# Scan stage: segment decays turned round into two fp32r parts made on GpSimd, input products in three fp32r passes

## What is computed

```python
u = layernorm(u, x_norm_w, x_norm_b)                       # after the adaptive norm
zxbcdt = einsum('bld,od->blo', u, l2norm(in_proj_w)) * DIM ** -0.5
z, xBC, dt_raw = zxbcdt[..., :512], zxbcdt[..., 512:1152], zxbcdt[..., 1152:]
xBC = silu(causal_conv(xBC, conv_w, taps=4) + conv_b)      # x: 4 heads of 128, B and C: 64 each
dt = softplus(dt_raw + dt_bias);  A = -exp(A_log)
# per chunk
dA = dt * A;  cum = cumsum(dA)
decay[i, j] = exp(cum[i] - cum[j])  for j <= i, per head
y = (C B^T * decay * dt) x  +  C state exp(cum)  +  D x
state = state * exp(cum[-1]) + B^T (dt * exp(cum[-1] - cum) * x)
g = y * silu(z);  out = rmsnorm(g) @ l2norm(out_proj_w).T
```

## Time and profile before

| | |
|---|---|
| median of 3 runs | 5127.16 us (5111.26 to 5134.68) |
| span of the profiled execution | 5138.9 us |
| attention | 262.7 to 2922.3 us |
| first mixture | 2928.5 to 3606.2 us |
| scan, with its set-up | 3618.3 to 4510.0 us |
| route and second mixture | 4516.0 to 5130.7 us |
| busy over the span | PE 92%, DVE 83%, ACT 68%, POOL 27% |

### The profile page before, as it was taken

How to read it: one execution, slowest core, us unless ns; L and a number is a source line. 1 busy time by engine, 2 the same in 40 slices (tenths; PEclk the granted TensorE clock), 3 DMA queues, 4 the chain that set the end, 5 groups by cost and what they waited for, 6 DMA issues and landing times. The chain is left out here.

```text
span 5138.9 us, 109366 instructions
## 1 busy us (share of the span) xinstructions
PE 4706.1 (92%) x35413; PEld 2589.8 (50%) x35413; DVE 4275.5 (83%) x6882; ACT 3471.8 (68%) x6677; POOL 1377.0 (27%) x1279
## 2 busy tenths in 40 slices
PE   5869999999999999999999689999599999955998
PEld 4723333333333333333333267777366666645887
DVE  5779999999999999999999768878677877775554
ACT  2428888888888888888888523223377877734554
POOL 1111111111111111111111133333234443435776
PEclk8969999999999999999999889999699999956999
DMA  4931222212222122221222211111100000044442
GB/s 153 349 67 35 52 52 46 43 35 53 52 46 43 35 53 51 46 43 38 50 54 43 71 40 37 41 45 37 53 21 27 25 23 28 21 156 164 166 160 92
DMA packets 236717, 340.13 MB, mean 66 GB/s; under 512 B 60215, under 2 KB 170034, under 8 KB 227612
## 3 DMA queue, kind: packets, MB, share of 16 engines
q1 hardware_dynamic: 220032, 275.39, 22.3%
q0 software_dynamic: 16192, 58.43, 3.1%
HBM read 205.62 MB, written 136.18 MB: 67 GB/s over the span
## 5 line engine op out<-in xcount | busy, mean ns | idle before, releaser
L719 DVE TENSOR_REDUCE at_mxp<-at_ps_m 128x2 f32<-128x1024 f32 x2092 | 2524.4, 1221 | 70.2 <-PE at_ps_m L772 47.3
L692 ACT ACTIVATE at_prob<-at_ps_s 128x512 f32<-128x512 f32 x4100 | 2227.3, 596 | 323.5 <-PE at_ps_s L762 299.7
L782 PE MATMUL at_ps_o<-at_prob,at_vs 128*32 128x256 f32 x16384 | 1313.1, 392 | 13.9 <-ACT at_osum L698 13.9
L762 PE MATMUL at_ps_s<-at_qs,at_ks 51*128 51x512 f32 x4100 | 1036.7, 500 | 2.7 <-ACT at_prob L692 2.7
L772 PE MATMUL at_ps_m<-at_ks,at_qs 49*128 49x512 f32 x4184 | 859.0, 406 | 49.8 <-DMA at_ks<-t_alibi 34.4
L762 PEld LDWEIGHTS at_ps_s<-at_qs,at_ks 51*128 51x128 f32 x4100 | 384.6, 183 | 853.3 <-ACT at_prob L692 852.8
L782 PEld LDWEIGHTS at_ps_o<-at_prob,at_vs 128*32 128x32 f32 x16384 | 322.9, 108 | 778.2 <-issue 389.7
L564 POOL TENSOR_TENSOR at_total<-at_total,at_minus 128x16 f32<-128x16 f32 x65 | 189.6, 2917 | 1128.4 <-DMA at_total<-at_osum 1128.4
L772 PEld LDWEIGHTS at_ps_m<-at_ks,at_qs 49*128 49x128 f32 x4184 | 403.7, 190 | 73.7 <-DVE at_mxp L719 38.0
L67 DVE TENSOR_TENSOR ex_hidc<-ex_hid,ex_hidc 128x512 fp32r<-128x512 f32 x128 | 158.5, 1250 | 169.6 <-ACT ex_hid L2550 169.6
L1222 PE MATMUL mi_ps_f<-mi_w,mi_act 128*128 128x256 f32 x1024 | 260.1, 399 | 17.4 <-DVE mi_acc L1072 17.1
(11 more groups left out here) (317 smaller groups left out, 6161.6 us busy)
## 6 DMA issues: line engine op xcount, KB each, us to landing
t_parts<-pr_parts SPq DMA_DIRECT2D x64, 512.0 KB, 6.4
ex_w<-in_fw SPq DMA_DIRECT2D x32, 1024.0 KB, 7.4
at_ks<-t_parts SPq DMA_DIRECT2D x102, 256.0 KB
t_buf<-at_blank POOLq DMA_DIRECT2D x64, 384.5 KB, 3.2
at_qs<-t_parts SPq DMA_DIRECT2D x96, 256.0 KB
at_vs<-t_v SPq DMA_DIRECT2D x17, 1024.0 KB, 4.8
ex_rest<-t_buf SPq DMA_DIRECT2D x16, 1026.0 KB, 5.2
t_v<-pr_vaug SPq DMA_DIRECT2D x64, 256.0 KB, 5.6
```

The costliest lines, as they stand in the source:

```text
L692: nc.scalar.activation(prob[0 if up is None else (t + 1) % 2][:, j, :], ps_s[bank][:, :], ACT.Exp).then_inc(s_read, 1)
L719: nc.vector.tensor_reduce(out[:, s4, k + i, 2 * pair:2 * pair + 2], ps_m[i][:, :, :], AX.X, ALU.max).then_inc(mx_read, 1)
L762: nc.tensor.matmul(ps_s[bank][:, :], ks[s][a:a + QROWS, j // 2, t1 * P:(t1 + 1) * P], qs[s][a:a + QROWS, j // 2, c * T:(c + 1) * T], start ...
L782: last = nc.tensor.matmul(ps_o[32 * j:32 * j + 32, q0:q1], vs[s][:, t, 32 * j:32 * j + 32], prob[t % 2][:, j, q0:q1], start=(t == 0 and ha ...
```

## The change

1. **Decays** (`segment_mask`, `decays`). The roles of the factors are turned round: `lowerc`, an fp32r copy of `lower`, is stationary, and the moving factor is `upper * dA` for all four heads side by side, 512 columns. It is made in two fp32r parts from an upper and a lower part of `dA` (`step_parts`, five drains and four small operations). The masks move from ACT (four 128x128 operations) to GpSimd (two 128x512 operations). TensorE then does two fp32r matmuls of 512 columns in place of four fp32 ones of 128.
2. **Gates and convolution inputs.** `uTc[h]` and `winc` hold fp32r upper and lower parts. Each of the 18 products per turn of 512 columns is three fp32r passes. ACT now writes both `uTc[h][0]` and the fp32 `uT` (one buffer, read by `steps`); GpSimd makes the lower part (`lower_rows`). The weights are cut once, in the set-up: ACT the upper parts, GpSimd the lower.
3. **In place.** The convolution works in `xs[h]`; the tile `cv` is gone.

The diff, cut to its core:

```diff
-        win = sb("win", [P, KD, ZX])
+        wdt = sb("wdt", [P, KD, NH])
+        winc = [sb(f"winc{c}", [P, KD, RT * P], F32R) for c in range(2)]
...
-        uT = [sb(f"uT{h}", [P, KD, T]) for h in range(2)]
+        uT = sb("uT", [P, KD, T])
+        uTc = [[sb(f"uTc{h}{c}", [P, KD, T], F32R) for c in range(2)] for h in range(2)]
...
-        cv = sb("cv", [P, CTL, T])
...
+                def step_parts(h):
+                    pool.drain()
+                    nc.gpsimd.tensor_scalar(dA_big[:, :, :], dA[h][:, :, :], 4097.0, None, ALU.mult)
+                    pool.drain()
+                    nc.gpsimd.tensor_tensor(dA_off[:, :, :], dA_big[:, :, :], dA[h][:, :, :], ALU.subtract)
+                    pool.drain()
+                    nc.gpsimd.tensor_tensor(dAc[h][0][:, :, :], dA_big[:, :, :], dA_off[:, :, :], ALU.subtract)
+                    pool.drain()
+                    lower_part(nc.gpsimd, dAc[h][1][:, :, :], dA[h][:, :, :], dAc[h][0][:, :, :])
+                    pool.drain()
+
+                def segment_mask(h, s, used):
+                    if used is not None:
+                        pool.wait_ge(a_done, used + 1)
+                    for c in range(2):
+                        last = nc.gpsimd.tensor_tensor(segc[s % 2][c][:, :, :], upper[:, :].unsqueeze(1).to_broadcast([P, NH, P]),
+                                                       over_h(dAc[h][c][:, s, :].bitcast(F32)), ALU.mult)
+                    last.then_inc(seg_set, 1)
+
+                def lower_rows(turn, h, k, name):
+                    pool.wait_ge(a_out, place(turn, name)[0] + 1)
+                    lower_part(nc.gpsimd, uTc[h][1][:, k, :], uT[:, k, :], uTc[h][0][:, k, :]).then_inc(u_cut, 1)
...
                         second_root(i + 2)
+                        segment_mask(h, 3, place(turn, "seg1")[0])
                         if c == 0:
                             weigh_rows(b, i)
                         softplus_argument(i + 1)
                         softplus_series(i + 1, 1 - h)
                         gate(i, h, 1, old)
+                        step_parts(1 - h)
+                        segment_mask(1 - h, 0, place(turn, "seg2")[0])
                         gate(i, h, 2, True)
+                        segment_mask(1 - h, 1, place(turn, "seg3")[0])
                         gate(i, h, 3, True)
+                        lower_rows(turn, h, 0, "uT0")
+                        segment_mask(1 - h, 2, place(turn, "seg0")[0])
+                        lower_rows(turn, h, 1, "uT1")
...
-                    for k in range(NH):
-                        last = nc.scalar.activation(segm[s % 2][:, k, :], lower[:, :], ACT.Copy, scale=dA[h][:, s, k:k + 1])
-                    last.then_inc(seg_set, 1)
...
-                    nc.scalar.activation(uT[h][:, k, :], bank[:, :], ACT.Identity, scale=nw[:, k:k + 1], bias=nb[:, k:k + 1]).then_inc(a_out, 1)
+                    nc.scalar.activation(uTc[h][0][:, k, :], bank[:, :], ACT.Identity, scale=nw[:, k:k + 1], bias=nb[:, k:k + 1])
+                    nc.scalar.activation(uT[:, k, :], bank[:, :], ACT.Identity, scale=nw[:, k:k + 1], bias=nb[:, k:k + 1]).then_inc(a_out, 1)
...
+                act.wait_ge(w_read, 5)
+                for j in range(5):
+                    nc.scalar.copy(win_part(0, j), win_f[j]).then_inc(win_upper, 1)
...
+                    if ct == 4:
+                        pe.wait_ge(u_cut, KD if i is None else KD * (i[0] + 2))
...
-                        last = nc.tensor.matmul(bank[:, :], win[:, k, DI + ct * P:DI + (ct + 1) * P], uT[h][:, k, :], start=(k == 0), stop=(k == KD - 1))
+                        for n, (a, r) in enumerate(CUTS):
+                            last = nc.tensor.matmul(bank[:, :], winc[a][:, k, DI + ct * P:DI + (ct + 1) * P], uTc[h][r][:, k, :],
+                                                    start=(k == 0 and n == 0), stop=(k == KD - 1 and n == 2))
...
-                    for k in range(NH):
-                        last = nc.tensor.matmul(bank[:, k * P:(k + 1) * P], segm[s % 2][:, k, :], upper[:, :], start=True, stop=True)
+                    for c in range(2):
+                        last = nc.tensor.matmul(bank[:, :], lowerc[:, :], segc[s % 2][c][:, :, :].rearrange("p h c -> p (h c)"), start=(c == 0), stop=(c == 1))
```

More of the change, by code:

```diff
@@ L1319, in scan_phase @@
         two = lambda name, shape: [sb(f"{name}{h}", shape) for h in range(2)]
-        segm, decay, att = two("segm", [P, NH, P]), two("decay", [P, NH, P]), two("att", [P, NH, P])
+        decay, att = two("decay", [P, NH, P]), two("att", [P, NH, P])
+        segc = [[sb(f"segc{h}{c}", [P, NH, P], F32R) for c in range(2)] for h in range(2)]
+        dAc = [[sb(f"dAc{h}{c}", [P, SUB, NH], F32R) for c in range(2)] for h in range(2)]
+        dA_big, dA_off = sb("dA_big", [P, SUB, NH]), sb("dA_off", [P, SUB, NH])
+        lowerc = sb("lowerc", [P, P], F32R)
         sm, btw, ex = two("sm", [P, P]), two("btw", [P, NH, NS]), two("ex", [P, 3, SUB, NH])
@@ L1356, in scan_phase @@
         RND = 7
+        WIN_PIECES = [(8, 9), (4, 6), (6, 8), (0, 2), (2, 4)]
+        win_part = lambda c, j: winc[c][:, :, WIN_PIECES[j][0] * P:WIN_PIECES[j][1] * P]
+        win_f = [(osb[0] if j == 0 else sz[1])[:, :, :].rearrange("p s c -> p (s c)")[:, a % 8 * D:a % 8 * D + KD * (b - a) * P].rearrange("p (k c) -> p k c", k=KD)
+                 for j, (a, b) in enumerate(WIN_PIECES)]
         over_h = lambda v: v.unsqueeze(2).to_broadcast([P, NH, P])
@@ L1471, in batch @@
                         h = c % 2
+                        turn = (i, c)
                         old = c > 0 or not first
@@ L1493, in _ @@
                 second_root(0)
+                for j in range(3):
+                    lower_weights(j)
                 first_root(1)
+                for k in range(KD):
+                    lower_rows(None, 0, k, f"uT{k}")
+                for j in range(3, 5):
+                    lower_weights(j)
                 pool.wait_ge(setup_v, 3)
@@ L1498, in _ @@
                 second_root(1)
+                pool.wait_ge(const_in, NCONST)
+                step_parts(0)
+                segment_mask(0, 0, None)
+                segment_mask(0, 1, None)
+                for k in range(KD):
+                    lower_rows(None, 1, k, f"vT{k}")
+                segment_mask(0, 2, place(None, "seg0")[0])
                 pool.wait_ge(w_read, RND)
-                pool.wait_ge(const_in, NCONST)
                 batch(0, True)
@@ L1693, in _ @@
                 dve.wait_ge(const_in, NCONST)
+                nc.vector.tensor_copy(lowerc[:, :], lower[:, :]).then_inc(lower_cut, 1)
                 for r in range(RND):
@@ L1842, in batch @@
                         steps(turn)
-                        segment_mask(i, h, 3, place(turn, "seg1")[0])
                         decays(turn, i, 1, old)
@@ L1858, in batch @@
                         decays(turn, i, 3, True)
-                        segment_mask(i + 1, 1 - h, 0, place(turn, "seg2")[0])
                         projected(turn, h, 0)
@@ L1864, in batch @@
                         decays(turn, i + 1, 0, True)
-                        segment_mask(i + 1, 1 - h, 1, place(turn, "seg3")[0])
                         gates(turn, 1 - h, 2)
@@ L1881, in batch @@
                         projected(turn, h, 3)
-                        segment_mask(i + 1, 1 - h, 2, place(turn, "seg0")[0])
                         skip_inputs(turn, i + 1, 1 - h, 0, True)
@@ L1909, in conv_inputs @@
                 def conv_inputs(i, h, ct):
+                    if i is None:
+                        pe.wait_ge(win_cut, {4: 1, 0: 2, 1: 2, 2: 3, 3: 3}[ct])
+                    if ct == 4:
+                        pe.wait_ge(u_cut, KD if i is None else KD * (i[0] + 2))
                     bank = into(i, f"ct{ct}")
                     for k in range(KD):
[L1912 removed]
+                        for n, (a, r) in enumerate(CUTS):
+                            last = nc.tensor.matmul(bank[:, :], winc[a][:, k, DI + ct * P:DI + (ct + 1) * P], uTc[h][r][:, k, :],
+                                                    start=(k == 0 and n == 0), stop=(k == KD - 1 and n == 2))
                     last.then_inc(a_done, 1)
                 def gates(i, h, s):
+                    if i is None:
+                        pe.wait_ge(win_cut, 5)
                     bank = into(i, f"z{s}")
                     for k in range(KD):
[L1918 removed]
+                        for n, (a, r) in enumerate(CUTS):
+                            last = nc.tensor.matmul(bank[:, :], uTc[h][a][:, k, s * P:(s + 1) * P], winc[r][:, k, 0:DI],
+                                                    start=(k == 0 and n == 0), stop=(k == KD - 1 and n == 2))
                     last.then_inc(a_done, 1)
@@ L1924, in steps @@
                         for k in range(KD):
-                            last = nc.tensor.matmul(bank[:, s * NH:(s + 1) * NH], uT[h][:, k, s * P:(s + 1) * P], win[:, k, RT * P:ZX], start=(k == 0), stop=(k == KD - 1))
```

(1 more changed line is left out.)

33 lines of the change are left out of this document (15 added, 18 removed).

## The result

The changed kernel takes **5212.7 us** (median of 4 runs, 5206.0 to 5230.1), the kernel before, run beside it, 5123.8. The ratio is 1.0181, with a 95% interval of 1.0159 to 1.0202: 89 us slower. The forecast was 5247 us and slower, so the direction and the range hold and the size is 31 us too large.

A forecast was written before the change was run, and what follows sets the result against it. TensorE bounds the scan, but GpSimd's chain has no slack and would pace it after the change: 27.0 + 30.5 = 57.5 us a turn against 50.3, loop +116, set-up +4, so 5247 us, 2.3% slower; range 5160 to 5315.

The forecast's parts named there:

- the 2.41 us behind `wob`: TensorE's wait for the gate in a batch's first turn, where GpSimd also makes `wob`; read as GpSimd's chain lacking slack.
- its own signs: Profile signs named beforehand for the forecast being right (TensorE's waits, clock, turn length, operation durations) or wrong.
- the lock-out: In the scan's tail, GpSimd's run of four operations, 5.0 us, holds DVE's `attention_weights(0)` back until 17.8.
- Leg A: GpSimd's chain in a scan turn, from the start of gate 0 to the end of mask 0; 27.0 us.
- Leg B: The rest of the scan turn, from the end of mask 0 to the next gate 0; 30.5 us.
- TensorE to the end of the fourth gate product: First part of the stretch after mask 0: 7.1 us of work plus 2.5 for half clock, 9.6.
- rival A: GpSimd paces the loop, but DVE gets in between its operations and TensorE keeps its clock; 5157 us, 10%.
- DVE's chain from there to gate 0: From `attention_weights(0)` to the end of `own_outputs(0)`, 12.6 us, then the gate 0.15 later; `own(0)` done before.
- TensorE's saving: Faster products in the scan: 3.3 us from gates and convolution inputs, 2.0 from decays, together 5.3 us a turn.
- The ten operations: GpSimd's added 128x512 operations per scan turn, priced from the gate (1.27 us) and the mixture's lower parts.
- B: Rival: faster, the softplus chain gets short and A holds as well; a turn 48.5 us, 5103 us, 7%.
- C: Rival: TensorE stays the bound, all GpSimd work in its shadow; 85 us less, 5046 us, 3%.

The follow-up runs named there:

- e3: The changed kernel with the mask of block 3 made ahead of gate 0 instead of behind it; 5182.8 us, ratio 1.0136.
- e7: The changed kernel with mask 3 and `wob` ahead of gate 0 and the second root behind mask 0; 5164.0 us, ratio 1.0063.
- e8: e7 with the softplus argument also moved ahead of gate 0, and `step_exp` earlier on ACT; 5097.7 us, ratio 0.9950.
- e11: The kernel before, only reordered: `wob` and softplus argument ahead of gate 0, second root behind gate 1, `step_exp` earlier on ACT; 5102.9 us, ratio 0.9956.
- e6: The changed kernel with useless matmuls filling TensorE's two waits, 18 ahead of gate 1's transposes, 6 ahead of `decays(0)`; 5165.5 us, ratio 1.0076.

## Why the prediction was right, and where its size was off

**What bounds the kernel.** Right. GpSimd's chain is the bound once anything is added (e3, e7, e8), and the 2.41 us behind `wob` were the sign of it. I put the kernel before down as bound by TensorE; that holds but for the first turn of each batch, where the order alone gave back 21 us (e11).

**Against its own signs.** Of what was to show it, the two waits in every turn came, and a granted clock near 0.85 (0.87). The rest did not: TensorE was busy 87% of the loop for 75 to 80, turns took 54.5 us for 57 to 58, masks 1.10 in the mean for 1.25 to 1.3, and `attention_weights` 0.79 in the mean (0.73 before) for 2 or more. The last was named as the sign that kills the lock-out. That the time still fell into the range is in part luck: the lock-out and the masks were priced too high, what is listed below as missing stood against them.

**Leg A, 27.0 forecast, 25.8 measured.** Root 3.1 (4266.16 to 4269.26) as forecast; mask 3 2.0 for 2.5; softplus 15.5 for 15.9; gate 1 and parts 3.15 for 3.0; mask 0 2.0 for 2.5. The term that was mis-sized is the mask: I took the gate's 1.27, it was 1.02.

**Leg B, 30.5 forecast, 28.8 measured**, from errors of opposite sign:

- TensorE to the end of the fourth gate product: 9.6 forecast, 9.5 measured, 2.2 of it the lower clock for the 2.5 that I took (e6). ACT's second column operation is done at 12.2, as forecast, and the first lower part starts there too, beside DVE's third convolution group (4301.32 to 4304.71), where the forecast had made it wait until 12.8. It paid for it with 1.72 us.
- The lock-out of DVE: `attention_weights` at 17.8 forecast, at 14.5 (4306.43) measured. **This step failed.** It was read from one place in another stage; in the scan DVE got in behind the operation under way. Its 14.5 is where rival A with the clock's loss has it (12.8 + 1.8).
- DVE's chain from there to gate 0: 12.7 forecast, 14.3 measured. I had written that `own(0)` is done before. It is not: DVE waits 1.39 us for it at 4319.86, since TensorE, late itself, is at the lower clock for a second time in its twelve passes (4.22 us, 3.06 in e6).

**Sum.** 54.5 a turn for 57.5, and 77 us on the loop for 116; the set-up +6 for +4. Over 16 times 54.5 the loop has 25 us more, where I had put 16 for `wob` and the first turn. The rest is leg B ahead of the next batch, 31.9, 32.1 and 30.3 us where others take some 28.7; the forecast had nothing for it, and no run asks why.

**TensorE's saving.** 5.3 us a turn forecast. The input products gave 2.8 for 3.3 (six passes take 1.48, not 1.40: 4250.92 to 4252.33 is the best case, 1.41). The decays' two passes take 0.57 (4250.35 to 4250.92) for 0.98, so 0.4 a block and 1.6 for 2.0. Only the few products of leg B lie on the path; the rest of the saving is in TensorE's waits.

**The ten operations.** I took 12.5 us, and in the turn shown they take 11.6 (2.04, 2.04, 2.04, 2.48, 1.72, 1.26). At 1.12 us an operation, an estimate from the 4497 ns for 2048 elements of the Trainium skill ("GPSIMD Engine Reference", section 3.1), they would come to 11.2, and the estimate of the time from it, 5225, came nearer than my 5247; but undisturbed, none was at 1.12, which lies between the 1.02 and the 1.27 of the rows. The advice in section 4.1 of that page to keep such operations off GpSimd holds here, for the masks.

**The rivals.** A's first half, DVE let in, came true without its second, the clock kept: 5197 was its figure, and 5213 was measured. Its turn, 27.0 + 27.4 = 54.4, is the one measured, by luck: the masks made leg A 1.2 us shorter, the second stretch at the lower clock and the wait for `own(0)` made leg B 1.4 longer. What it lacks is the time ahead of the batches and in the set-up. With both (e6, where the clock was kept by force) the time is 5165 for A's 5157. B needed the softplus chain short by itself. It stayed at 15.5, and less of it stood in leg A only when its first part was moved ahead of gate 0 (e8); that e8's 5098 is near B's 5103 says nothing for B. C, TensorE still the bound, fell with the profile: it waits 107 us for GpSimd (79.5 and 27.4).
